# Sampling rows of four images interleaved on every fourth partition

## The chip, the cores and the metric

The kernel runs on one core of one Trainium2 chip. The metric is the device time of one execution in microseconds; the time before is the median of three runs.

## The reference, cut to what matters

A tower of vision layers over 32 images: a tokenizer made of a deformable convolution, then four pairs of attention and feed-forward layers with layer norms. Only the tokenizer matters here. Each image is cut into a 5 x 5 grid of patches of 16 x 16 points; a small convolution gives every point an offset, and the image is read at the displaced place with bilinear weights:

```python
off = _conv_offsets(x, offset_w, offset_b)            # dy, dx for 256 points of 25 patches
py = base_y[None, :, None, :] + dy
px = base_x[None, None, :, :] + dx
y0 = jnp.floor(py)
x0 = jnp.floor(px)
...
sampled = gather(y0i, x0i) * (wy0 * wx0)[..., None] + gather(y0i, x1i) * (wy0 * wx1)[..., None] + gather(y1i, x0i) * (wy1 * wx0)[..., None] + gather(y1i, x1i) * (wy1 * wx1)[..., None]
out = jnp.einsum('bhwkc,ock->bohw', sampled, Wk)
```

## The kernel before

The kernel is one program of nine stages with a barrier of all engines between them. The tokenizer is stage 0 and has three parts: `offsets` computes the places, `sample` reads the images at them, `project_and_norm` multiplies with `dconv`. The change is in `sample` and in a constant of `layout`.

`sample` writes the bilinear weight as a product of two hats, max(0, 1 - |place - row|) over the rows and the same over the columns. It goes through 40 steps: five rows of patches (`ho`) times eight tiles (`t`) of four images. A step has a window of 20 image rows for each of its four images (`WINDOW` = 20, `IMG_PER_TILE` = 4, `ROWS_Y` = 80), and each of these 80 rows is one partition. The parts of a step, by line:

- L1691, SP: the transfer of places. The y places of a row of patches, 5 x 256 numbers (5,120 B) per image, were stored to device memory by `offsets`; they are brought to the 80 partitions of `hat_y`, each image's numbers repeated for its 20 rows.
- L1696, SP: four transfers of strips, one per image: 20 rows of 3 x 84 pixels (1,008 B) each. `strip` has a slot per image in the free dimension, and image `j`'s rows fill only its own slot on its own 20 partitions; the rest stays zero from a memset at the start. So one matmul with the 80 rows as contraction keeps the four images apart.
- L1714 and L1719, ACT: the hat of y in two operations on 80 partitions. The first subtracts the row's number in its window, which is the constant `minus_row`, one number for each partition. L1717 and L1721, ACT: the same for x, after a subtraction by POOL at L1734.
- L1752, PE: 20 matmuls of hat y with the strips, into one of two sets of PSUM banks.
- L1783 and L1791, DVE: the product with the hat of x (two instructions), and the sum.

`hat_y` and `strip` have four buffers: SP waits at L1688 until the matmuls of the step four back are done, then issues the five transfers of its step, one after the other. ACT waits for the places, PE for the hat, for all four strips and for DVE to have read the bank of two steps back. Every engine has its own loop over the steps, and there is no barrier between steps. The far branch (L1698, L1703) isn't taken with these inputs.

Of the kernel before, what the change touches and what calls it, by code (L numbers as in the profile page):

```python
# [17 lines left out]
QUAD = 32  # L18
IMG_PER_TILE = 4
P = QUAD * IMG_PER_TILE  # L20
# [1468 lines left out]
GRID = 5  # L1489
TILE_TOKENS = IMG_PER_TILE * TOKENS  # L1490
KPOINTS = PATCH * PATCH
# [6 lines left out]
WINDOW = PATCH + 2 * MARGIN  # L1498
# [8 lines left out]
ROWS_Y = IMG_PER_TILE * WINDOW  # L1507
# [121 lines left out]
def sample(tw, k, w):  # L1629
# [12 lines left out]
    loads = {kind: {x: [tw.sem(f"{kind}_{x}_loaded_{p}") for p in range(BUFFERS)] for x in ("places", "pixels")} for kind in (NEAR, FAR)}  # L1642
# [12 lines left out]
    def near_or_far(eng, step, before_far=None):  # L1655

        far = eng.value_load(k.far[0:1, 0:1], min_val=0, max_val=1)
        with eng.If(far == 0):
            one_pass(eng, lambda *a: step(NEAR, *a), 0, 0, 0)
        with eng.Else():  # L1660
            if before_far:
                before_far()
            with eng.Fori(0, COVER_Y) as wy:
                with eng.Fori(0, COVER_X) as wx:
                    one_pass(eng, lambda *a: step(FAR, *a), (wy * COVER_X + wx) * (GRID * TILES), wy, wx)
# [6 lines left out]
    with tw.scratch():  # L1672
# [9 lines left out]
        with nc.psum_tensor("ps_rows", [P, 2, 4, 512], F32) as ps, nc.Block() as block:  # L1682

            @block.sync
            def _(sp):
                def step(kind, i, ho, t, p, wy, wx):
                    n = B + i + 1
                    sp.wait_ge(sems[kind]["rows_in_psum"], n - BUFFERS)  # L1688
                    version = 0 if kind == NEAR else wy + 1
                    places = k.rel_d[version].rearrange("(t j h w) c -> t h j (w c)", t=TILES, j=IMG_PER_TILE, h=GRID)[t][ho]  # L1690
                    sp.dma_start(hat_y[0:ROWS_Y, p].rearrange("q w c -> q (w c)"),  # L1691
                                 places.unsqueeze(1).to_broadcast([IMG_PER_TILE, WINDOW, GRID * KPOINTS])).then_inc(loads[kind]["places"][p], 16)
                    for j in range(IMG_PER_TILE):
                        q = slice(WINDOW * j, WINDOW * (j + 1))
                        if kind == NEAR:
                            sp.dma_start(strip[q, p, j], ins["strips"][ho][t][j]).then_inc(loads[kind]["pixels"][p], 16)  # L1696
                        else:
                            sp.dma_start(window[q, p, j], ins["windows"][wy][wx][t][j]).then_inc(loads[kind]["pixels"][p], 16)  # L1698

                def store_places():  # L1700
                    for wy in range(COVER_Y):
                        sp.wait_ge(moved, wy + 1)
                        sp.dma_start(k.rel_d[1 + wy].rearrange("(t n) c -> n t c", n=TILE_TOKENS), moved_places).then_inc(saved, 16)  # L1703
                    sp.wait_ge(saved, 16 * COVER_Y)

                near_or_far(sp, step, store_places)
# [1206 lines left out]
def layout(x):  # L2913

    a = {k: np.asarray(v) for k, v in x.items()}
    o = {}
# [3 lines left out]
    p = x[:, :, :GRID * PATCH, :GRID * PATCH].reshape(IMAGES, CHANNELS, GRID, PATCH, GRID, PATCH)  # L2920
# [16 lines left out]

    place = o["base"].reshape(TILE_TOKENS, 2, KHALVES, P)
    o["origin"] = np.concatenate([place[:, 0, 0:1, 0], place[:, 1, :, 0]], 1) - MARGIN
    o["minus_row"] = -np.resize(np.arange(WINDOW, dtype=np.float32), P)[:, None]  # L2940
    column, half = np.arange(WINDOW_X), np.arange(KHALVES)
    o["window_x"] = np.tile(HALF_COLS * half[:, None, None] + PATCH * g[:, None] - MARGIN + column, (P, 1, 1, 1)).astype(np.float32)
    o["cover_x"] = np.tile(WINDOW_X * np.arange(COVER_X)[:, None] + column, (P, 1, 1)).astype(np.float32)
# [120 lines left out]
```

## Time and profile before

| | us |
|---|---|
| median of three runs | 1320.39 (1316.8 to 1324.31) |
| time of the profiled execution | 1309.12 |
| its span | 1307.5 |
| sampling loop in it | from about 72 to 257 |

A row of a profile is a group of like instructions, a single one, or a stretch of time; the line number is that of the code above. "Idle before" is the time for which an engine stood before an instruction, with what released it. All times are microseconds unless marked ns. SPq is the sequencer of SP, which issues the transfers and computes nothing; its row of a transfer is the time for which the sequencer was taken up by the issue, not the time of the transfer.

### The profile page before, as it was taken

Reading aid. Unit: us, or ns where it says so; the run is one execution under the profiler, and the core shown is the slowest. Engines: PE = TensorE matmul, PEld = TensorE weight load, DVE = VectorE, ACT = ScalarE, POOL = GpSimd, SP = SyncE. Lnnn points to the kernel's source line nnn. Section 1 sums busy time; section 2 is a strip of 40 time slices with the busy share of each in tenths; the row PEclk is TensorE's granted clock in tenths of the full one; section 3 lists DMA queues with packets and bytes.
Section 4 is the critical chain, followed back from the end, with each engine's and each line's share of the span. In section 5 each row is a group of like instructions: output and inputs, shape, how many; then the busy total and the mean of one; then the engine's idle time right before and its main releaser. Section 6 shows DMA issues by size and latency. Waiting matters only on the chain. (4 is left out here: it accounts for less than half of the span.)

```text
span 1307.5 us, 25828 instructions
## 1 busy us (share of the span) xinstructions
PE 903.5 (69%) x9931; PEld 739.1 (57%) x9931; DVE 636.0 (49%) x1464; ACT 427.5 (33%) x728; POOL 215.1 (16%) x240
## 2 busy tenths in 40 slices
PE   4936666654656469828988557857677999476684
PEld 1335555522333359726878556646447999464573
DVE  1637777636776343166444233645463111256354
ACT  0148888512333112123334322334220111133132
POOL 2122222110000134213112001010012332100100
PEclk9969999976665579968888758968586999879598
DMA  4323333276000358010000060000052996100000
GB/s 120 83 87 113 115 114 114 79 191 145 1 0 1 98 174 204 19 49 2 2 2 2 1 156 9 4 1 3 1 133 68 225 256 144 32 2 3 1 4 20
DMA packets 63923, 90.67 MB, mean 69 GB/s; under 512 B 16532, under 2 KB 51016, under 8 KB 63824
## 3 DMA queue, kind: packets, MB, share of 16 engines
q1 hardware_dynamic: 58320, 83.57, 23.4%
q0 software_dynamic: 5504, 5.70, 2.2%
q8 instruction: 72, 1.18, 0.4%
q14 instruction: 27, 0.22, 0.1%
HBM read 81.66 MB, written 8.12 MB: 69 GB/s over the span
## 5 line engine op out<-in xcount | busy, mean ns | idle before, releaser
L1752 PE MATMUL ps_rows<-stage_strip,stage_hat_y 128*128 128x144 f32 x800 | 110.4, 294 | 73.1 <-ACT stage_hat_y L1719 73.1
L1752 PEld LDWEIGHTS ps_rows<-stage_strip,stage_hat_y 128*128 128x128 f32 x800 | 102.1, 193 | 81.4 <-ACT stage_hat_y L1719 50.1
L1783 DVE TENSOR_TENSOR stage_product<-ps_rows,stage_hat_x 128x1296 f32<-128x1296 f32 x80 | 68.9, 902 | 42.8 <-PE ps_rows L1752 42.8
L2559 DVE TENSOR_TENSOR L_ffnhid<-L_ffnact_gate,L_ffnbank_u 128x300 f32<-128x300 f32 x32 | 15.0, 467 | 117.6 <-ACT L_ffnact_gate L2577 117.6
L1791 DVE TENSOR_REDUCE stage_samples<-stage_product 128x1440 f32 x40 | 66.2, 1655 | 9.3 <-DVE stage_product L1783 9.3
L1714 ACT ACTIVATE stage_hat_y<-stage_hat_y,stage_w_minus_row 80x1280 f32<-80x1280 f32 x40 | 54.5, 1362 | 45.8 <-DMA stage_hat_y<-places_y 45.8
L1734 POOL TENSOR_TENSOR stage_hat_x<-stage_pos_xT,stage_w_window_x 128x240 f32<-128x240 f32 x80 | 48.4, 627 | 125.0 <-DVE stage_product L1783 118.9
L1556 PE MATMUL ps_conv<-stage_w_offset_w,stage_patches 128*100 128x512 f32 x96 | 44.8, 620 | 17.6 <-DMA stage_patches<-in_patchesT 17.6
L1719 ACT ACTIVATE stage_hat_y<-stage_hat_y 80x1280 f32<-80x1280 f32 x40 | 50.1, 1253 | 0.0
L1135 PE MATMUL L_attnbank_q<-L_attnhT,L_attnwq 97*128 97x200 f32 x192 | 43.6, 374 | 6.9 <-DVE L_attnqT L1298 6.7
L1135 PEld LDWEIGHTS L_attnbank_q<-L_attnhT,L_attnwq 97*128 97x128 f32 x192 | 36.8, 213 | 9.4 <-issue 8.7
L2523 PE MATMUL L_ffnbank_g<-L_ffnxT,L_ffn_win 96*128 96x100 f32 x240 | 40.7, 297 | 0.5 <-ACT L_ffnxT L2570 0.5
L2523 PE MATMUL L_ffnbank_u<-L_ffnxT,L_ffn_win 96*128 96x100 f32 x240 | 40.7, 297 | 0.0
L2492 POOL DMA_INDIRECT stage_y_rows<-L_ffndown,stage_choice_index x16 | 25.5, 1594 | 89.0 <-ACT L_ffndown L2584 89.0
L2577 ACT ACTIVATE L_ffnact_gate<-L_ffnbank_g 128x300 f32<-128x300 f32 x32 | 13.5, 421 | 80.1 <-PE L_ffnbank_u L2523 80.1
L1556 PEld LDWEIGHTS ps_conv<-stage_w_offset_w,stage_patches 128*100 128x100 f32 x96 | 16.2, 175 | 40.8 <-issue 23.1
L2343 DVE TENSOR_TENSOR L_ffnhid<-L_ffnact_gate,L_ffnbank_u 128x480 f32<-128x480 f32 x16 | 10.5, 654 | 55.4 <-ACT L_ffnact_gate L2367 55.4
L1174 PE MATMUL L_attnbank_o<-L_attnv_heads,L_attnwork 128*100 128x68 f32 x192 | 25.8, 312 | 16.1 <-ACT L_attnwork L1422 14.9
L2523 PEld LDWEIGHTS L_ffnbank_g<-L_ffnxT,L_ffn_win 96*128 96x128 f32 x240 | 35.6, 213 | 0.8 <-issue 0.8
L2523 PEld LDWEIGHTS L_ffnbank_u<-L_ffnxT,L_ffn_win 96*128 96x128 f32 x240 | 35.6, 213 | 0.0
L1174 PEld LDWEIGHTS L_attnbank_o<-L_attnv_heads,L_attnwork 128*100 128x100 f32 x192 | 24.6, 223 | 18.1 <-ACT L_attnwork L1422 16.0
L2291 PE MATMUL L_ffnbank_g<-L_ffnxT,L_ffn_win 96*128 96x240 f32 x128 | 33.0, 382 | 0.7 <-ACT L_ffnxT L2360 0.7
(430 smaller groups left out, 2176.3 us busy)
## 6 DMA issues: line engine op xcount, KB each, us to landing
stage_hat_y<-places_y SPq DMA_DIRECT2D x40, 400.0 KB
L_ffn_win<-in_L_ffn_Win SPq DMA_DIRECT2D x10, 1152.0 KB, 8.9
stage_L_ffn_win<-in_L_ffn_Win SPq DMA_DIRECT2D x6, 1152.0 KB, 9.2
L_ffnranks<-stage_ranks SPq DMA_DIRECT2D x16, 400.0 KB
L_ffn_win<-in_L_ffn_Win SPq DMA_DIRECT2D x8, 768.0 KB, 14.0
L_ffn_wout<-in_L_ffn_Wout SPq DMA_DIRECT2D x10, 576.0 KB, 6.3
stage_L_ffn_wout<-in_L_ffn_Wout SPq DMA_DIRECT2D x6, 576.0 KB, 6.5
stage_strip<-in_strips SPq DMA_DIRECT2D x160, 19.7 KB
```

The costliest lines, as they stand in the source:

```text
L1135: mm = nc.tensor.matmul(bank_q[:, i * PAIR_TOKENS:(i + 1) * PAIR_TOKENS], wq[0:rows, k, c * GROUPS + g, :], tokens, start=(k == 0), stop=( ...
L1174: mm = nc.tensor.matmul(bank_o[0:QUERIES, j // 2, at:at + OUT_COLS], work[:, t % 2, j * GROUPS + g, :], v_heads[:, t % 4, j, g, :, :], sta ...
L1556: mm = nc.tensor.matmul(ps_conv[0:TILE_TOKENS, p, :], patches[:, p, c, :], w["offset_w"][:, c, :], start=(c == 0), stop=(c == SLABS - 1))
L1714: nc.scalar.activation(y, y, ACT.Abs, bias=w["minus_row"][0:ROWS_Y, :]).then_inc(s["hat_y_abs"], 1)
L1719: nc.scalar.activation(y, y, ACT.Relu, scale=-1.0, bias=1.0).then_inc(s["hat_y"], 1)
L1734: x = nc.gpsimd.tensor_tensor(hat_x[:, p, h * GRID * IMG_PER_TILE:(h + 1) * GRID * IMG_PER_TILE, :].rearrange("q (g j) x -> q g j x", j=IM ...
L1752: mm = nc.tensor.matmul(ps[:, p % 2, bank, at * cols:(at + 1) * cols], hat_y[:, p, g, h * P:(h + 1) * P], rhs.rearrange("q j c x -> q (j c ...
L1783: last = nc.vector.tensor_tensor(split(product[:, p % 2, slots.start * cols:slots.stop * cols]), ps[:, p % 2, banks, 0:used * cols].rearra ...
L1791: nc.vector.tensor_reduce(into.rearrange("q h c w -> q h w c"), by_window, AX_X, ALU.add).then_inc(s["summed"], 1)
L2291: mm = nc.tensor.matmul(ps[:, c, f, :], weights.win[e % NB][:, k, o:o + P], xT[:, e % 2, k, :], start=(k == 0), stop=(k == 1))
L2492: nc.gpsimd.indirect_dma_start(choice.y_rows, bass.IndirectOffsetOnAxis(choice.index[0:C, e:e + 1], 0), down[:, e % RING, :], None, bounds ...
L2523: mm = nc.tensor.matmul(ps[:, c, f, :], weights.win[e % NB][:, k, o:o + P], xT[:, e % 2, k, :], start=(k == 0), stop=(k == 1))
```

## The change

The rows of the four images are interleaved: partition `4 w + j` holds row `w` of image `j`, where before it was partition `20 j + w`. In the source of the transfer of places the dimension of 20 repeats stands outside that of the four images. Each image's strip goes to every fourth partition, and `minus_row` counts 0, 0, 0, 0, 1, 1, 1, 1 and so on. `hat_y` and the slots of `strip` keep their shapes.

```diff
--- before.py
+++ after.py
@@ -1689,9 +1689,9 @@
                     version = 0 if kind == NEAR else wy + 1
                     places = k.rel_d[version].rearrange("(t j h w) c -> t h j (w c)", t=TILES, j=IMG_PER_TILE, h=GRID)[t][ho]
                     sp.dma_start(hat_y[0:ROWS_Y, p].rearrange("q w c -> q (w c)"),
-                                 places.unsqueeze(1).to_broadcast([IMG_PER_TILE, WINDOW, GRID * KPOINTS])).then_inc(loads[kind]["places"][p], 16)
+                                 places.unsqueeze(0).to_broadcast([WINDOW, IMG_PER_TILE, GRID * KPOINTS])).then_inc(loads[kind]["places"][p], 16)
                     for j in range(IMG_PER_TILE):
-                        q = slice(WINDOW * j, WINDOW * (j + 1))
+                        q = slice(j, ROWS_Y, IMG_PER_TILE)
                         if kind == NEAR:
                             sp.dma_start(strip[q, p, j], ins["strips"][ho][t][j]).then_inc(loads[kind]["pixels"][p], 16)
                         else:
@@ -2937,7 +2937,7 @@
 
     place = o["base"].reshape(TILE_TOKENS, 2, KHALVES, P)
     o["origin"] = np.concatenate([place[:, 0, 0:1, 0], place[:, 1, :, 0]], 1) - MARGIN
-    o["minus_row"] = -np.resize(np.arange(WINDOW, dtype=np.float32), P)[:, None]
+    o["minus_row"] = -np.repeat(np.arange(QUAD, dtype=np.float32), IMG_PER_TILE)[:, None]
     column, half = np.arange(WINDOW_X), np.arange(KHALVES)
     o["window_x"] = np.tile(HALF_COLS * half[:, None, None] + PATCH * g[:, None] - MARGIN + column, (P, 1, 1, 1)).astype(np.float32)
     o["cover_x"] = np.tile(WINDOW_X * np.arange(COVER_X)[:, None] + column, (P, 1, 1)).astype(np.float32)
```

The order of the instructions on every engine is the same as before. The instructions of the transfers in the built program differ in their patterns (step and number of elements of each dimension, outermost first) and, for the strips, in a field `ant_dge_precooked`, which is printed here where it is set:

```
before
L1691 out [[5120, 80], [1, 1], [1, 1280]]  in [[6400, 4], [0, 20], [1, 1280]]
L1696 out [[4032, 20], [1, 252]]           in [[252, 20], [1, 252]]            ant_dge_precooked
after
L1691 out [[5120, 80], [1, 1], [1, 1280]]  in [[0, 20], [6400, 4], [1, 1280]]
L1696 out [[16128, 20], [1, 252]]          in [[252, 20], [1, 252]]
```

All other transfers that SP issues in either program have that field set, except those of the far branch at L1698. Among them are the two of later stages that the rows below show: L2227 brings one row of 800 numbers (3,200 B) to 128 partitions, L2410 brings 128 rows of six pieces.

## Rows read from the trace of the kernel before

**Rows 1.** Busy time by stretch: the sampling loop, and 20 us in it.

```profile
core 0: us, PE busy (x) PEld busy (x) DVE busy (x) ACT busy (x) POOL busy (x), PEclk, DMA share, GB/s
...
72.00:256.00 184.00, 110.41 (x800) 102.07 (x800) 133.70 (x120) 140.32 (x160) 48.35 (x80) 0.96 0.30 107
110.00:130.00 20.00, 12.33 (x92) 11.26 (x91) 15.75 (x14) 16.85 (x19) 5.39 (x9) 1.00 0.31 114
```

**Rows 2.** Groups of the sampling loop: busy us, mean ns, idle before and releaser.

```profile
L1752 PE MATMUL ps_rows<-stage_strip,stage_hat_y 128*128 128x144 f32 x800 | 110.4, 294 | 73.1 <-ACT stage_hat_y L1719 73.1
...
L1783 DVE TENSOR_TENSOR stage_product<-ps_rows,stage_hat_x 128x1296 f32<-128x1296 f32 x80 | 68.9, 902 | 42.8 <-PE ps_rows L1752 42.8
L1791 DVE TENSOR_REDUCE stage_samples<-stage_product 128x1440 f32 x40 | 66.2, 1655 | 9.3 <-DVE stage_product L1783 9.3
L1714 ACT ACTIVATE stage_hat_y<-stage_hat_y,stage_w_minus_row 80x1280 f32<-80x1280 f32 x40 | 54.5, 1362 | 45.8 <-DMA stage_hat_y<-places_y 45.8
```

**Rows 3.** Timeline of ACT (start, duration): first step, one in the middle, last.

```profile
79.91 1.36 ACT L1714 ACTIVATE stage_hat_y<-stage_hat_y,stage_w_minus_row 80x1280 f32<-80x1280 f32 x1 [14.95 <-DMA stage_hat_y<-places_y]
...
152.87 1.36 ACT L1714 ACTIVATE stage_hat_y<-stage_hat_y,stage_w_minus_row 80x1280 f32<-80x1280 f32 x1 [0.79 <-DMA stage_hat_y<-places_y]
...
155.80 0.59 ACT L1721 ACTIVATE stage_hat_x<-stage_hat_x 128x480 f32<-128x480 f32 x1
157.17 1.36 ACT L1714 ACTIVATE stage_hat_y<-stage_hat_y,stage_w_minus_row 80x1280 f32<-80x1280 f32 x1 [0.78 <-DMA stage_hat_y<-places_y]
...
247.57 1.36 ACT L1714 ACTIVATE stage_hat_y<-stage_hat_y,stage_w_minus_row 80x1280 f32<-80x1280 f32 x1 [0.80 <-DMA stage_hat_y<-places_y]
```

**Rows 4.** DMA view of 72 to 256 us: packets and issues.

```profile
DMA packets 8167, 19.69 MB, mean 107 GB/s; under 512 B 1760, under 2 KB 4960, under 8 KB 8160
...
stage_hat_y<-places_y SPq DMA_DIRECT2D x40, 400.0 KB
stage_strip<-in_strips SPq DMA_DIRECT2D x160, 19.7 KB
```

**Rows 5.** Waits of SP in 72 to 256 us: total us, times, longest.

```profile
SPq L1691 <- PE ps_rows L1752: 40.8, 35, 2.7
```

**Rows 6.** Timeline of SP, the transfer issues at the start of the loop.

```profile
72.14 0.86 SPq L1691 DMA_DIRECT2D stage_hat_y<-places_y  x1
...
75.41 0.70 SPq L1691 DMA_DIRECT2D stage_hat_y<-places_y  x1
...
78.95 0.71 SPq L1691 DMA_DIRECT2D stage_hat_y<-places_y  x1
79.92 1.72 SPq L1696 DMA_DIRECT2D stage_strip<-in_strips  x4
81.96 0.68 SPq L1691 DMA_DIRECT2D stage_hat_y<-places_y  x1
```

**Rows 7.** Transfer issues of SP by line: count, then ns min/median/max.

```profile
L1691 SPq DMA_DIRECT2D stage_hat_y<-places_y x40: 671/677/861, 72.1 to 236.4; - x40
...
L1696 SPq DMA_DIRECT2D stage_strip<-in_strips x160: 286/286/344, 73.3 to 238.7; - x160
...
L2227 SPq DMA_DIRECT2D L_ffnranks<-stage_ranks x16: 319/428/437, 453.0 to 493.8; - x16
...
L2410 SPq DMA_DIRECT2D L_ffn_wout<-in_L_ffn_Wout x10: 367/368/3597, 763.0 to 1091.8; - x10
```

**Rows 8.** Timeline of DVE: first product, two without a wait, last product.

```profile
88.09 1.72 DVE L1783 TENSOR_TENSOR stage_product<-ps_rows,stage_hat_x 128x1296 f32<-128x1296 f32 x2 [17.91 <-PE ps_rows L1752]
...
91.55 1.71 DVE L1783 TENSOR_TENSOR stage_product<-ps_rows,stage_hat_x 128x1296 f32<-128x1296 f32 x2
...
95.09 1.71 DVE L1783 TENSOR_TENSOR stage_product<-ps_rows,stage_hat_x 128x1296 f32<-128x1296 f32 x2
...
253.45 1.72 DVE L1783 TENSOR_TENSOR stage_product<-ps_rows,stage_hat_x 128x1296 f32<-128x1296 f32 x2 [0.67 <-PE ps_rows L1752]
```

**Rows 9.** Busy time by stretch, while only four L2227 transfers run.

```profile
456.00:458.00 2.00, 0.00 (x0) 0.00 (x0) 0.00 (x0) 0.00 (x0) 0.00 (x0) 0.50 0.91 230
```

## The prediction

> **What bounds the kernel now.** I read four views of the sampling loop, the only place where the change acts, in this order: the stretches, the groups, the DMA view, and the issues of SP.
>
> The stretches say where the loop lies and that no engine in it is full: 184 us, of which ACT is busy 140.3 and DVE 133.7, and from 110 us on TensorE holds its full granted clock [rows 1]. The groups say who waits for whom: DVE waits for PE (42.8 us), PE for ACT's hat of y (73.1), and ACT's first operation of a step, L1714, waits in all 40 steps for the transfer of places (45.8) [rows 2]. The timeline of ACT gives the beat: L1714 starts at 79.91 in the first step and at 247.57 in the last, so a step is 167.66 / 39 = 4.30 us. ACT's four operations end 3.52 us after L1714 starts (155.80 + 0.59 - 152.87), and then it stands 0.78 us until the next transfer has landed [rows 3]. So the transfers of places set the beat.
>
> Why does one need 4.30 us? The transfer at L1691 brings 80 rows of 5,120 B and the four of L1696 bring 20 rows of 1,008 B each. Over 40 steps that is 3,200 and 3,200 data packets. The DMA view counts 8,160 under 8 KB and 4,960 under 2 KB, which fits with 1,760 left over, all under 512 B [rows 4]. 1,760 = 40 x 4 + 160 x 10: one closing packet for each DMA engine that takes part, if a transfer of places runs on 4 engines and a strip on 10. I know no other split that fits (40a + 160b = 1,760 with a and b dividing the 20 rows or the 4 images). The load agrees: at a share of 0.31 of 16 engines [rows 1] a step has 0.31 x 16 x 4.30 = 21.3 engine-us; four engines busy all the time are 17.2 of them, and the other 4.1 on six engines are 0.7 each, which is the strips' part. On the four engines places then take 4.30 - 0.7 = 3.6 us, 0.18 us a packet.
>
> [...]
>
> **The change, part by part.**
>
> *Transfer of places.* Its outer dimension becomes 20. If it runs on 10 engines, as the strips with 20 rows do, each takes 8 of its packets: 8 x 0.18 = 1.44 us, with the strips 2.1 us a step on each engine. The DMA engines no longer bound anything. The first transfer lands 12 x 0.18 = 2.1 us earlier. From its issue at 72.14 [rows 6] to L1714 at 79.91 [rows 3] were 7.8 us; 5.7 remain.
>
> *Next in line: DVE.* Where it had no wait its steps were 3.46 us (88.09 to 91.55) and 3.54 (91.55 to 95.09) [rows 8]; with ACT at about 3.5 the loop could run at 3.52.
>
> *Next in line: SP.* SP issues five transfers a step and waits 40.8 us in 35 waits for PE to free a buffer [rows 5], 1.17 us a step. Its own work is therefore 4.30 - 1.17 = 3.13 us; the one steady interval without a wait, 78.95 to 81.96, is 3.01 [rows 6]. This is only 1.17 us below the present beat, and less than DVE's 3.52 by 0.4.
>
> *Strips.* And here the change takes something away. Their destination was 20 neighbouring partitions; it becomes every fourth. In the built program the four strip transfers lose the field `ant_dge_precooked`, which all SP transfers but L1691's and the unused far branch's carry. The number of bytes, rows and instructions is the same, the form of the issue isn't. The trace has prices for both forms, though for different shapes: L1696 with the mark costs SP 286 ns, L1691 without it 677 [rows 7]. Lower bound: nothing, 286 stays. Upper bound: 677, so 0.39 us more for each strip. How much of the 0.39 is shape? [...] That leaves 0.25 us for the mark, and I take it: 4 x 0.25 = 1.00 us a step. The transfer of places was unmarked and stays so; for six more engines I add the 0.03 between the marked 286 and 319.
>
> SP's step is then 3.13 + 1.00 + 0.03 = 4.16 us. That is more than DVE's 3.52, so SP sets the beat. Its first two intervals were longer than its own 3.13, by 0.14 and 0.41 (3.27 and 3.54 [rows 6]); I keep 0.5.
>
> The last L1714 starts at 72.14 + 39 x 4.16 + 0.5 + 5.7 = 240.6 instead of 247.57: 7.0 us earlier. What follows it (8.5 us to the end of the loop, then the projection) is unchanged.
>
> *The rest.* ACT's bias per row is another table of the same size, the matmuls contract over the same 80 rows in another order, no instruction moves on any engine: nothing. PE would run at the same clock and wait.
>
> **Sum.** The profiled execution took 1309.12 us; less 7.0 is 1302.1. The median of the three timed runs is 11.3 us above that execution, so the forecast on their scale is 1320.4 - 7.0 = 1313.4 us, 0.5% faster. A measurement of this kernel can tell about 0.5% (6.6 us) from no change.
>
> **The rivals.**
>
> *A. The mark costs nothing on SP.* Then DVE sets the beat at 3.52. The first product starts 2.1 us earlier, at 86.0, the last at 86.0 + 39 x 3.52 = 223.3 instead of 253.45 [rows 8]: 30.2 us, 1290 us. For it: SP's time shows no dependence on the mark alone, since no two rows have one shape. Against: 286 and 677 are the two ends of all SP issues in the loop, and they are split by exactly this. [...]
>
> *B, on the other side: strips cost what L1691 costs.* Place: SP's sequencer at L1696. Price: 0.39 x 4 = 1.56 us, a step of 4.72, last L1714 at 72.14 + 184.1 + 0.5 + 5.7 = 262.4, 14.9 us later than now: 1335 us. It decides from the point where 72.14 + 39T + 6.2 passes 247.57, T = 4.34, which is 0.295 us more for each strip. For it: 677 is the only unmarked price the trace has. Against: L1691 has a third level and four times the rows.
>
> *C. The transfer stays on 4 engines.* Then the DMA beat of 4.30 remains, unless SP's is longer: 1320 us. Against: 10 engines for the strips' 20 rows.
>
> *D. Ten engines that read the same 20 KB get in each other's way.* The worst row: while only transfers that repeat one row of 3,200 B for 128 partitions run, 0.91 of 16 engines move 230 GB/s [rows 9], 15.8 B a ns each. A packet of places would take 0.32 us, eight 2.6 us, with strips 3.3: still under 4.16. To reach 4.30 it would have to be 0.45. So this costs up to 1 us at the first landing and no more; the time is the forecast's.
>
> **How the numbers follow.** Cases by the extra time of a strip issue: none or nearly (A): 0.11, about 1290. From 0.05 to 0.25 us: 0.37, times from 1295 to 1313. From 0.25 to 0.34: 0.29, within 0.5% of no change. Above: 0.20, to 1335 (B). C: 0.03. The forecast's own case, 0.20 to 0.30 us, has 0.40 of it all, and its own range is steps of 3.96 to 4.36, 1306 to 1321 us. For 8 in 10 I cut half of A and a third of B, and allow 3 us for the spread of the runs: 1292 to 1333. Faster by over 0.5%: 0.48; within: 0.31; slower: 0.21.
>
> **What would show it.** In the changed profile: packets under 512 B in the loop 40 x 10 + 160 x 10 = 2,000 (1,760 if C). The mean of L1696's issues at about 0.54 us (0.29 for A, 0.68 for B), that of L1691 at about 0.7. SP's wait for PE gone, where now it is 1.17 us a step; if it is still there and ACT no longer waits for DMA, A. L1714 of the first step at about 77.8. Steps of 4.16 us. ACT's idle time would still be put down to DMA, although the DMA engines are idle more, because a transfer issued late lands late: the DMA share stays near 21 / (16 x 4.16) = 0.32. The prediction is wrong if the strips' issue is off by more than 0.05 us, since each 0.05 is 0.2 us a step and 7.8 us in all; that is the number on which everything hangs.

## The result and the profile after

The changed kernel takes 1350.78 us (median of 4 runs, 1350.23 to 1354.24) against 1322.35 for the kernel before: ratio 1.0271, 95% interval 1.0225 to 1.0317. This ratio isn't the quotient of the two medians, which are 28.4 us apart and give 1.0215. The kernel is thus 2 to 3% slower, where 0.5% faster was forecast.

The issues of SP by line (count, then ns min/median/max), as in [rows 7]:

```profile
L1691 SPq DMA_DIRECT2D stage_hat_y<-places_y x40: 803/803/1025, 72.3 to 272.7; - x40
...
L1696 SPq DMA_DIRECT2D stage_strip<-in_strips x160: 727/741/772, 73.7 to 276.5; - x160
```

The strip issue is the number to read: 741 ns, where it was 286. The places' issue rose too, from 677 to 803. SP's timeline at the start of the loop (start, duration), as in [rows 6]:

```profile
72.35 1.02 SPq L1691 DMA_DIRECT2D stage_hat_y<-places_y  x1
...
77.62 0.80 SPq L1691 DMA_DIRECT2D stage_hat_y<-places_y  x1
...
83.11 0.80 SPq L1691 DMA_DIRECT2D stage_hat_y<-places_y  x1
84.16 3.55 SPq L1696 DMA_DIRECT2D stage_strip<-in_strips  x4
88.04 0.80 SPq L1691 DMA_DIRECT2D stage_hat_y<-places_y  x1
```

In this interval SP needs 4.93 us from one transfer of places to the next (83.11 to 88.04), where the steady one before took 3.01; the interval in front of it is longer (77.62 to 83.11, 5.49), and so the mean of the loop will be too. Within a step one strip's issue follows the other after (3.55 - 0.741) / 3 = 0.936 us; before it was (1.72 - 0.286) / 3 = 0.478. SP's waits in the whole loop:

```profile
engine line waited for: us in total, times, longest us
SPq L1682 <- PEq L1682: 11.5, 1, 11.5
```

The wait for PE at L1691, 40.8 us before [rows 5], is gone; what is left is the barrier at the end. So SP never stands: it sets the beat. The timeline of ACT, first step, last step, and the first instruction after the barrier at the loop's end:

```profile
77.69 1.36 ACT L1714 ACTIVATE stage_hat_y<-stage_hat_y,stage_w_minus_row 80x1280 f32<-80x1280 f32 x1 [12.54 <-DMA stage_hat_y<-places_y]
...
278.15 1.36 ACT L1714 ACTIVATE stage_hat_y<-stage_hat_y,stage_w_minus_row 80x1280 f32<-80x1280 f32 x1 [1.54 <-DMA stage_hat_y<-places_y]
...
289.36 1.28 ACT L1899 ACT_TABLE_LOAD   x1 [7.70 <-PEq L1682]
```

A step is (278.15 - 77.69) / 39 = 5.14 us, before 4.30 [rows 3]. The first L1714 starts 2.2 us earlier than before, as was expected of the faster transfer.

A second reading tells whether SP or the DMA engines set a beat: the time from the issue of a transfer of places to the L1714 that needs it. Before it was 7.8 us in the first step (72.1 to 79.91) and 11.2 in the last (236.4 to 247.57), so transfers queued up behind each other. Now it is 5.3 (72.35 to 77.69) and 5.5 (272.7 to 278.15): nothing queues up, and a transfer comes late only because it is issued late. The groups and two stretches of the loop (columns of the stretches as in [rows 1]):

```profile
L1752 PE MATMUL ps_rows<-stage_strip,stage_hat_y 128*128 128x144 f32 x800 | 136.9, 340 | 78.4 <-ACT stage_hat_y L1719 78.4
...
L1783 DVE TENSOR_TENSOR stage_product<-ps_rows,stage_hat_x 128x1296 f32<-128x1296 f32 x80 | 68.8, 901 | 75.4 <-PE ps_rows L1752 75.4
...
L1714 ACT ACTIVATE stage_hat_y<-stage_hat_y,stage_w_minus_row 80x1280 f32<-80x1280 f32 x40 | 54.5, 1362 | 76.2 <-DMA stage_hat_y<-places_y 76.2
```

```profile
72.00:289.36 217.36, 136.85 (x800) 128.48 (x800) 133.94 (x120) 140.32 (x161) 48.34 (x81) 0.81 0.38 91
110.00:130.00 20.00, 13.05 (x77) 12.22 (x76) 12.83 (x13) 13.06 (x17) 4.46 (x8) 0.83 0.41 98
```

ACT's wait is still put down to the transfer of places, now 76.2 us; DVE waits 75.4 for PE. TensorE's granted clock in those 20 us is 0.83 where it was 1.00, and a matmul takes 340 ns where it took 294. Between steps that costs nothing, since SP is late anyway; only the last step's chain, from L1714 to the end of the loop, takes 11.2 us where it took 9.8. The DMA view tells that the number of engines changed as planned:

```profile
DMA packets 8405, 19.67 MB, mean 95 GB/s; under 512 B 2000, under 2 KB 5200, under 8 KB 8400
```

2,000 packets under 512 B are 40 x 10 + 160 x 10: places now run on ten DMA engines. The records of the single packets agree: from the first to the last packet of places four were under way in 137 of 173 us before; now, of the 108 us in which any is under way, ten are in 75.

The loop ends at 289.36 instead of 257.37, 32.0 us later: 39 x 0.84 for the steps, less 2.2 at the first, and 1.4 more behind the last. The two profiled spans differ by 41.1. The other 9.1 us lie behind the loop, where nothing was changed: from the loop's end to the end of the span were 1050.1 us before and 1059.2 after, and in the traces of the runs below between 1051 and 1066. This time goes roughly with TensorE's granted clock, read from 700 to 1100 us: 1050 and 1051 us in the two traces with 0.80, 1055 to 1062 in the seven with 0.79, 1059 (the changed kernel's) and 1063 in the two with 0.78 and 1065.5 in the one with 0.77. Why the clock differs there was not tried. The loop's part, 32.0 us or 2.4%, is what the rest of this document explains; it lies between the 2.15% of the medians and the 2.7% of the ratio.

### The profile page after: what moved, and what is told of

It reads as the page before. It is cut to its first block and busy times, and to the rows that moved or that the text cites. A ratio compares the mean times of both kernels' runs of the same rounds, so it can differ in the third digit from the quotient of the medians.

```text
span 1348.6 us, 25828 instructions
## 1 busy us (share of the span) xinstructions
PE 945.3 (70%) x9931; PEld 777.4 (58%) x9931; DVE 635.2 (47%) x1464; ACT 427.4 (32%) x728; POOL 215.1 (16%) x240
## 5 line engine op out<-in xcount | busy, mean ns | idle before, releaser
L1752 PE MATMUL ps_rows<-stage_strip,stage_hat_y 128*128 128x144 f32 x800 | 136.9, 340 | 78.4 <-ACT stage_hat_y L1719 78.4
L1752 PEld LDWEIGHTS ps_rows<-stage_strip,stage_hat_y 128*128 128x128 f32 x800 | 128.5, 234 | 86.7 <-ACT stage_hat_y L1719 50.0
L1783 DVE TENSOR_TENSOR stage_product<-ps_rows,stage_hat_x 128x1296 f32<-128x1296 f32 x80 | 68.8, 901 | 75.4 <-PE ps_rows L1752 75.4
L1714 ACT ACTIVATE stage_hat_y<-stage_hat_y,stage_w_minus_row 80x1280 f32<-80x1280 f32 x40 | 54.5, 1362 | 76.2 <-DMA stage_hat_y<-places_y 76.2
```

The costliest lines, as they stand in the source:

```text
L1714: nc.scalar.activation(y, y, ACT.Abs, bias=w["minus_row"][0:ROWS_Y, :]).then_inc(s["hat_y_abs"], 1)
L1752: mm = nc.tensor.matmul(ps[:, p % 2, bank, at * cols:(at + 1) * cols], hat_y[:, p, g, h * P:(h + 1) * P], rhs.rearrange("q j c x -> q (j c ...
L1783: last = nc.vector.tensor_tensor(split(product[:, p % 2, slots.start * cols:slots.stop * cols]), ps[:, p % 2, banks, 0:used * cols].rearra ...
```

## The experiments

Theory M: the transfer of places alone would have freed the loop, but the strips lost the mark (the field `ant_dge_precooked`), and SP's issue time took over the beat.

**The mark alone.** The kernel before, with

```diff
+                            nc.dge_precook = False
                             sp.dma_start(strip[q, p, j], ins["strips"][ho][t][j]).then_inc(loads[kind]["pixels"][p], 16)
+                            nc.dge_precook = True
```

> The kernel before, with the strip transfers' destinations as they were (20 neighbouring partitions) and only the mark taken from their instructions; the transfer of places stays on 4 engines. Theory M (the lost mark): the strip issues go from 0.29 to about 0.74 us although nothing in their pattern changed, SP's step is 3.13 + 4 x 0.455 = 4.95 us, its wait for PE is gone, the last L1714 comes some 25 us later: ratio to the kernel before 1.019. Rival S (the stride): it is the step of four partitions that makes the issue or the write dear; here there is none, so the issue stays at 0.29, the step at 4.30, ratio 1.00.

Measured: 1349.64 us, ratio 1.0247 (1.0212 to 1.0283). Issues, and ACT's first and last step (the line of L1714 is L1716 here):

```profile
L1691 SPq DMA_DIRECT2D stage_hat_y<-places_y x40: 699/699/868, 70.9 to 268.7; - x40
...
L1697 SPq DMA_DIRECT2D stage_strip<-in_strips x160: 727/745/810, 72.1 to 272.5; - x160
```

```profile
78.51 1.36 ACT L1716 ACTIVATE stage_hat_y<-stage_hat_y,stage_w_minus_row 80x1280 f32<-80x1280 f32 x1 [14.75 <-DMA stage_hat_y<-places_y]
...
276.16 1.36 ACT L1716 ACTIVATE stage_hat_y<-stage_hat_y,stage_w_minus_row 80x1280 f32<-80x1280 f32 x1 [0.80 <-DMA stage_hat_y<-places_y]
```

The strip issue costs 745 ns with the old partitions, the step is 197.65 / 39 = 5.07 us (4.95 expected, and a ratio of 1.019). A loss of the same size comes with the mark alone; the stride of four partitions isn't needed for it. Rival S falls. That unmarked strips make the DMA engines late, and not SP, is excluded by the time from issue to L1716: 7.6 us in the first step (70.9 to 78.51) and 7.5 in the last (268.7 to 276.16), where it grew to 11.2 in the kernel before.

**Places alone.**

```diff
-                                 places.unsqueeze(1).to_broadcast([IMG_PER_TILE, WINDOW, GRID * KPOINTS])
+                                 places.unsqueeze(0).to_broadcast([WINDOW, IMG_PER_TILE, GRID * KPOINTS])
```

> The kernel before with only the pattern of the places transfer changed (20 outside 4); strips and minus_row are as before, so the hats are computed from rows of the wrong image and the output isn't the reference's. Theory M: the strips keep their mark, SP's step is 3.13 + 0.13 = 3.26 us, the places run on 10 engines, and DVE sets the beat at about 3.52 us: 30 us faster, ratio 0.977. Packets under 512 B in the loop: 2,000. Rival T (the transfer on ten engines is itself no faster, since all read the same 20 KB): steps of 4.3 us or more, ratio 1.00 or above.

Measured: 1284.89 us, ratio 0.9737 (0.9704 to 0.9769). Issues, SP's wait, 20 us of the loop (columns as in [rows 1]), ACT's first and last step:

```profile
L1691 SPq DMA_DIRECT2D stage_hat_y<-places_y x40: 812/814/1020, 72.4 to 206.5; - x40
...
L1696 SPq DMA_DIRECT2D stage_strip<-in_strips x160: 286/287/424, 73.8 to 209.0; - x160
```

```profile
SPq L1691 <- PE ps_rows L1752: 4.1, 13, 0.4
```

```profile
150.00:170.00 20.00, 15.05 (x113) 14.08 (x113) 18.55 (x18) 20.00 (x25) 7.28 (x12) 1.00 0.57 138
```

```profile
77.76 1.36 ACT L1714 ACTIVATE stage_hat_y<-stage_hat_y,stage_w_minus_row 80x1280 f32<-80x1280 f32 x1 [12.47 <-DMA stage_hat_y<-places_y]
...
212.18 1.35 ACT L1714 ACTIVATE stage_hat_y<-stage_hat_y,stage_w_minus_row 80x1280 f32<-80x1280 f32 x1
```

The step is 134.42 / 39 = 3.45 us, and ACT is busy 20.00 of 20 us: ACT sets the beat, a little below the 3.52 that I had read from DVE. The transfer on ten engines is worth 33 us. SP has almost nothing to spare: with 4.1 us of waits in all, 0.1 a step, its own work is about 3.35 us. Nor have the DMA engines: a share of 0.57 of 16 is 9.1 engines, if all of this runs on the same ten.

**Strips alone.** The changed kernel with the places transfer of before.

> The changed kernel with the places transfer as before (4 outside 20): strips on every fourth partition, unmarked; the hats meet rows of the wrong image, so the output isn't the reference's. Theory M: SP's step is that of the changed kernel less what the places issue gained, 5.14 - 0.13 = 5.01 us, L1691's issue is back at 0.68, ratio to before about 1.02. Theory S predicts the same time; together with e1 it tells the two apart. Rival U (places on ten engines and strips get in each other's way in the changed kernel): the step falls to about 4.3, ratio 1.00.

Measured: 1350.19 us, ratio 1.0236 (1.0188 to 1.0284).

```profile
L1691 SPq DMA_DIRECT2D stage_hat_y<-places_y x40: 699/699/868, 71.1 to 268.9; - x40
...
L1696 SPq DMA_DIRECT2D stage_strip<-in_strips x160: 727/745/810, 72.3 to 272.7; - x160
```

The step is 5.08 us (first L1714 at 78.60, last at 276.61), again with no growing queue (7.5 us from issue to L1714 in the first step, 7.7 in the last). Same as with the mark alone, stride or no stride. In the changed kernel ten engines instead of four thus make no difference to the time, since SP is the bound.

**What decides the price of an unmarked issue?** In the kernel before, only the row count of strips 1 to 3 was changed, so that they should run on 1, 16 and 10 engines; first with the mark (in this and the later cuts of code, `...` stands for what is left out, such as the branches and the semaphores):

```diff
-                            sp.dma_start(strip[q, p, j], ins["strips"][ho][t][j]) ...
...
+                            sp.dma_start(strip[WINDOW:2 * WINDOW - 1, p, 1], ins["strips"][ho][t][1][0:WINDOW - 1]) ...
...
+                            sp.dma_start(strip[2 * WINDOW:2 * WINDOW + 16, p, 2], ins["strips"][ho][t][2][0:16]) ...
...
+                            sp.dma_start(strip[3 * WINDOW:3 * WINDOW + 10, p, 3], ins["strips"][ho][t][3][0:10]) ...
```

> The kernel before; of the strips of images 1, 2 and 3 only 19, 16 and 10 of the 20 rows are brought (the missing pixels are left out of the result), each with a line of its own, all marked. 19 rows should run on 1 DMA engine, 16 on 16, 10 and 20 on 10. Read: the issue's price by engines in the marked form. Theory K (SP pays for each engine that it feeds): 0.006 us an engine, as between 0.286 on 10 and 0.319 on 16: 20 rows 0.29, 19 rows 0.23, 16 rows 0.32, 10 rows 0.29. Rival R (it pays by rows): falling from 20 to 10. The time stays near that of before.

Measured, in the order of 20, 19, 16 and 10 rows:

```profile
L1696 SPq DMA_DIRECT2D stage_strip<-in_strips x40: 300/300/344, 72.8 to 263.1; - x40
...
L1698 SPq DMA_DIRECT2D stage_strip<-in_strips x40: 229/230/249, 73.3 to 263.6; - x40
...
L1700 SPq DMA_DIRECT2D stage_strip<-in_strips x40: 321/2155/3708, 73.8 to 264.0; - x40
...
L1702 SPq DMA_DIRECT2D stage_strip<-in_strips x40: 286/286/335, 74.3 to 266.5; - x40
```

With the mark the issue goes by engines: 0.23 us for one, 0.29 to 0.30 for ten, 0.32 at least for sixteen. The median of 2.16 at sixteen is a stall of the issue, and the time (one run) was 1348.92 us, against my expectation: the step is 4.995 us, with SP almost never waiting for PE (1.6 us in all). Here the transfers do queue up: from the issue of places to ACT's first operation are 7.8 us in the first step (71.7 to 79.49) and 12.1 in the last (262.2 to 274.31). My estimate is that the one DMA engine that carries the 19 rows has the most work. If it also carries a quarter of the places and its part of the other strips, that is 20 packets of places at a median of 0.196 us and 2 + 19 + 1 + 1 = 23 of strips at 0.046, 4.98 us a step. What makes SP's issue stall was not shown.

The same with the mark taken from the strip transfers, as in the first experiment:

> The same four row counts with the mark taken from the strip transfers (pixels of images 1 to 3 left out as there). Theory K: the price in the unmarked form is a base and 0.021 us an engine, as between L1691's 0.677 on 4 engines and 0.803 on 10: 20 rows 0.74, 19 rows (1 engine) 0.55, 16 rows (16 engines) 0.87, 10 rows 0.74. Rival R (rows): 0.74, 0.73, 0.70, 0.64. Packets under 512 B in the loop: 40 x (4 + 10 + 1 + 16 + 10) = 1,640.

Measured (one run, 1355.97 us), same order:

```profile
L1697 SPq DMA_DIRECT2D stage_strip<-in_strips x40: 750/752/812, 72.9 to 266.6; - x40
...
L1699 SPq DMA_DIRECT2D stage_strip<-in_strips x40: 616/620/636, 73.9 to 267.6; - x40
...
L1701 SPq DMA_DIRECT2D stage_strip<-in_strips x40: 549/562/1602, 74.8 to 268.4; - x40
...
L1703 SPq DMA_DIRECT2D stage_strip<-in_strips x40: 795/801/811, 75.5 to 269.5; - x40
```

Here too the transfers queue up (7.5 us from issue to ACT in the first step, 71.7 to 79.15, and 11.6 in the last, 265.7 to 277.32), so this run's time says nothing of SP's part in it; only its issues are read. Four more row counts, in the same way:

> As the unmarked run with four row counts, now with 8, 12, 18 and 5 rows (8, 12, 9 and 5 DMA engines; the other pixels are left out of the result). So far unmarked: 0.55 us on 16 engines, 0.62 on 1, 0.75 and 0.80 on 10, which no straight line in engines or rows fits. Theory N (a number of engines that is a power of two is cheap): 8 rows about 0.58, the other three 0.7 to 0.8. Theory H (the price has a hump in the middle): 8, 9, 12 and 5 all between 0.65 and 0.8, without a step between 8 and 9.

Measured (one run, 1338.89 us), in the order of 8, 12, 18 and 5 rows:

```profile
L1697 SPq DMA_DIRECT2D stage_strip<-in_strips x40: 670/671/698, 72.6 to 265.3; - x40
...
L1699 SPq DMA_DIRECT2D stage_strip<-in_strips x40: 745/751/772, 73.5 to 266.2; - x40
...
L1701 SPq DMA_DIRECT2D stage_strip<-in_strips x40: 746/748/787, 74.4 to 267.1; - x40
...
L1703 SPq DMA_DIRECT2D stage_strip<-in_strips x40: 702/704/716, 75.4 to 268.1; - x40
```

The packets under 512 B in this loop are 1,520 = 40 x (4 + 8 + 12 + 9 + 5), which fits these numbers of engines. By DMA engines the unmarked issue costs 0.62 (1), 0.70 (5), 0.67 (8), 0.75 (9), 0.75 to 0.80 (10), 0.75 (12) and 0.56 us (16). Theory K's straight line is refuted (it asked for 0.55 on 1 and 0.87 on 16), and so is rival R by rows: 10 rows cost more than 20. N and H both miss as stated: eight engines cost 0.67 and not 0.58, and there is a step of 0.08 between 8 and 9 where H allowed none. What is left of N, that 1, 8 and 16 engines (0.56 to 0.67) are cheaper than 5, 9, 10 and 12 (0.70 to 0.80), fits every row of the strips, but the numbers of rows and of engines were changed together in these runs. Why sixteen is so cheap stays open.

**Sixteen rows in the changed kernel.**

```diff
-                            sp.dma_start(strip[q, p, j], ins["strips"][ho][t][j]) ...
+                            sp.dma_start(strip[j:16 * IMG_PER_TILE:IMG_PER_TILE, p, j], ins["strips"][ho][t][j][0:16]) ...
```

> The changed kernel with 16 of the 20 rows of each strip brought (the last four rows of each window are left out of the result), still on every fourth partition and unmarked, so that each strip runs on 16 engines. The issue should fall from 0.74 to about 0.56 us, SP's step from 5.14 by 4 x 0.18 to about 4.4 us, so the kernel comes back to near the time before: ratio 1.00 to 1.01. If instead the stride holds the loop up, or the number of rows has no part in it, the step stays near 5.1 and the ratio at 1.02 to 1.03.

Measured: 1313.27 us, ratio 0.9973 (0.9936 to 1.0011).

```profile
L1691 SPq DMA_DIRECT2D stage_hat_y<-places_y x40: 834/838/1027, 71.9 to 235.9; - x40
...
L1696 SPq DMA_DIRECT2D stage_strip<-in_strips x160: 495/496/584, 73.3 to 239.1; - x160
```

Still strided, still unmarked, but 0.50 us an issue instead of 0.74 (0.56 expected); the step falls to (241.10 - 77.88) / 39 = 4.19 us, and the loss is gone. The cheaper issues alone give 5.14 - 4 x 0.245 = 4.16. The edit also brings a fifth fewer strip rows, on 16 engines instead of 10, but nothing queued up in the changed kernel (5.3 and 5.5 us from issue to L1714), so less to transfer could not have moved the beat.

**Other ways to get the gain.** One strip transfer with its zeros from device memory, in the changed layout:

```diff
-                    for j in range(IMG_PER_TILE):
-                        q = slice(j, ROWS_Y, IMG_PER_TILE)
...
-                            sp.dma_start(strip[q, p, j], ins["strips"][ho][t][j]) ...
...
+                        sp.dma_start(strip[0:ROWS_Y, p], ins["wide_strips"][ho][t]) ...
```

> The changed kernel with the four strip transfers of a step made one: the strips lie in device memory with their zeros, 80 rows of 4,032 B, and one marked transfer brings them to 80 neighbouring partitions. SP issues two transfers a step instead of five: about 0.80 + 0.26 + 0.35 + 0.35 = 1.8 us of its own, so it waits for PE again. Places on 10 engines take 1.44 us, strips on up to 16 engines 5 packets each, some 0.7 us. Theory M: DVE sets the beat at about 3.52, 30 us faster than before, ratio 0.977. Rival: four times the strip bytes (323 KB a step) make the DMA engines the bound, steps above 4 us, ratio 0.99 to 1.00.

Measured: 1302.57 us, ratio 0.9893 (0.9846 to 0.9940). SP's wait, and 20 us of the loop:

```profile
SPq L1691 <- PE ps_rows L1752: 74.7, 36, 5.3
```

```profile
150.00:170.00 20.00, 15.28 (x116) 14.21 (x116) 17.82 (x18) 18.91 (x22) 6.35 (x11) 1.00 0.80 196
```

SP waits again, 36 times and 2.1 us each time, and the step is (229.48 - 77.95) / 39 = 3.89 us, not 3.52. The rival named the right bound, though its steps were to be above 4 us: in this trace a packet of places takes 0.33 us on average and one of the wide strips 0.28. If places run on ten engines and strips on sixteen (1,040 packets under 512 B fit that), an engine that carries both needs 8 x 0.33 + 5 x 0.28 = 4.0 us a step. Four times the strip bytes use up most of what the ten engines gave.

With the old partitions, the places in four marked transfers:

```diff
...
+                    for j in range(IMG_PER_TILE):
+                        sp.dma_start(hat_y[WINDOW * j:WINDOW * (j + 1), p].rearrange("q w c -> q (w c)"),
+                                     places[j:j + 1].to_broadcast([WINDOW, GRID * KPOINTS])).then_inc(loads[kind]["places"][p], 16)
```

> The kernel before with the partitions as they were and the places brought by four transfers, one per image: 20 repeats each, marked, on 10 engines. SP issues eight marked transfers a step: 8 x 0.478 + 0.33 = 4.15 us and no unmarked one. Theory M (the mark and the number of issues set SP's step): 4.15 against 4.30, 6 to 8 us faster, ratio 0.995. Rival (ten engines alone give the gain): 3.45 us as with places changed alone, ratio 0.974.

Measured: 1306.39 us (10 runs), ratio 0.9943 (0.9913 to 0.9972).

```profile
76.24 1.36 ACT L1715 ACTIVATE stage_hat_y<-stage_hat_y,stage_w_minus_row 80x1280 f32<-80x1280 f32 x1 [11.75 <-DMA stage_hat_y<-places_y]
...
237.54 1.36 ACT L1715 ACTIVATE stage_hat_y<-stage_hat_y,stage_w_minus_row 80x1280 f32<-80x1280 f32 x1 [0.25 <-DMA stage_hat_y<-places_y]
```

161.30 / 39 = 4.14 us a step, 4.15 expected: eight marked issues, each 0.478 us behind the one before it, and 0.33 for the rest. And with the strips of two images in one transfer as well (`pair_strips`, 40 rows of 2,016 B, twice a step):

> As the last, and the strips brought by two transfers instead of four: 40 rows of two images with the zeros between them from device memory, 2,016 B a row. SP issues six marked transfers: 6 x 0.478 + 0.33 = 3.2 us, under ACT's 3.45. The strip bytes are 161 KB a step, half those of the single wide transfer. Theory M: ACT sets the beat, 3.45 to 3.6 us, ratio 0.975 to 0.98. Rival: the DMA engines bound it as with the wide transfer, 3.9 us, ratio 0.99.

Measured: 1285.07 us, ratio 0.9796 (0.9728 to 0.9863).

```profile
150.00:170.00 20.00, 15.06 (x113) 13.96 (x112) 18.56 (x18) 20.00 (x25) 7.25 (x12) 1.00 0.59 165
```

```profile
77.69 1.36 ACT L1717 ACTIVATE stage_hat_y<-stage_hat_y,stage_w_minus_row 80x1280 f32<-80x1280 f32 x1 [12.04 <-DMA stage_hat_y<-places_y]
...
212.05 1.35 ACT L1717 ACTIVATE stage_hat_y<-stage_hat_y,stage_w_minus_row 80x1280 f32<-80x1280 f32 x1
```

ACT is full, the step is 134.36 / 39 = 3.45 us. This version computes all that the kernel before does and is faster than both kernels, by 2.0% than the one before and by some 4.6% than the changed one (0.9796 / 1.0271 = 0.954, from two sets of runs).

## Why the prediction was wrong

- *The transfers of places on four DMA engines bound the loop*: right. With places alone changed the time is 33 us shorter, and the packet count moved from 1,760 to 2,000 with the engines. Every count fits one packet under 512 B for each engine of a transfer, with 10 engines for 20 rows, and 1, 16 and 10 for 19, 16 and 10 rows (1,640 in both of those runs, as expected). These counts are sums over all transfers; the engines of a single strip transfer were not read by themselves.
- *The first transfer lands 2.1 us earlier*: 77.69 against 77.8 forecast.
- *Ten engines, 2.1 us a step on each, packets of 0.18 us*: wrong, without weight in the changed kernel. In its trace a packet of places takes 0.32 us on average (0.20 before), so an engine needs 8 x 0.32 + 8 x 0.08 = 3.2 us a step. That is Rival D's price almost to the digit (0.32 a packet, 3.3 a step). D was right, too, that it decides nothing at SP's beat; but with places alone changed (0.32 a packet again) it lies only 0.2 us under ACT's 3.45. For the same reason the DMA share came out at 0.38 over the loop; the 21 engine-us that the forecast put into 0.32 would give 0.26 at steps of 5.14 us. That the ten engines disturb each other over the same 20 KB, as D has it, was not tried.
- *SP next in line, 3.13 us of its own*: right. 3.13 + 4 x 0.455 + 0.126 = 5.08 us, measured 5.14.
- *The strips lose the mark, and SP sets the beat*: right as a mechanism, shown by the kernel with the mark alone removed.
- *0.25 us for each strip, at most 0.39*: the step that failed, and the term that was mis-sized. It is 0.455 (741 ns less 286), above even the upper bound. Of the 37.5 us by which the last L1714 comes later than forecast (278.15 against 240.6), this term is 39 x 4 x 0.205 = 32. I had taken L1691's 677 ns as a ceiling because its pattern is larger, and then taken 0.14 of the 0.39 off for shape, an amount that no run shows: with the pattern left as it was and the mark alone taken off, the issue rose by 0.459 us (745 ns less 286). But L1691 ran on four DMA engines and the strips on ten, and I had not asked what that is worth in the unmarked form. L1691 itself went to 803 ns with ten. Seen so, the strips' 741 is 677, with 126 more for the engines and 62 less for shape. This split isn't clean: L1691's pattern changed with its engines, and shape counts in its own right, since on ten engines each 10 rows cost 0.80 us and 20 rows 0.75. On sixteen engines the extra would have been 0.18 to 0.24 (0.50 or 0.56 less the marked 0.32), near my 0.25.
- *0.03 us for the places' issue on ten engines*: 0.126. Here I did go by engines, but at the marked form's price of 0.006 us an engine (L2227's least issue of 319 ns [rows 7] less 286, over six engines).
- *DVE's 3.52 as the floor*: it is ACT's 3.45. This had no weight. In the chances, 1295 us does not follow for 0.05 us more a strip: SP's step would be 3.36 us, under that floor, and the time Rival A's 1290.
- *PE at the same clock*: its granted clock fell from 1.00 to 0.83, which in the loop shows only in the 1.4 us behind the last step.
- Rival B had the right sign, place and mechanism with 4.72 us a step; with 5.14 it missed by 39 x 0.42 = 16 us. The range stopped short of even its time.

## What to carry to other kernels

A change of layout for the sake of one transfer can change the form of its neighbours' issue, as the strips' went from 286 to 741 ns here: compare the built instructions of every transfer on the queue, fields included, and not only their order and size. When an engine's sequencer has little slack (1.17 us a step for four issues: 0.29 us each here), an unknown price that is bounded by a row of another engine count isn't bounded. To tell a late issue from a slow transfer, compare the time from issue to use in the first and the last step: it grew from 7.8 to 11.2 us where transfers queued up, and stood at 5.3 and 5.5 where SP was late. Where one transfer must run on more engines, splitting it can leave the layout, and so its neighbours' mark, alone. The split costs more issues (here 4 x 0.478 = 1.9 us a step in place of one unmarked issue of 0.8 us), and pays in full only if they are won back elsewhere, as the paired strips did.

## What was not expected of the hardware

The unmarked issue's price over the number of DMA engines doesn't rise evenly (0.62 us on 1, 0.75 to 0.80 on 9 to 12, 0.50 to 0.56 on 16), while the marked one, read on 1, 10 and 16, rises from 0.23 over 0.29 to 0.32 at least. The DMA engines' busy time isn't a property of the packets alone: for the same 8,160 packets a step took 0.31 x 16 x 4.30 = 21.3 engine-us before, and 0.35 x 16 x 5.07 = 28 with the strips unmarked; with places on ten engines (8,400 packets) 0.57 x 16 x 3.45 = 31. There it is the places' own packets of 5,120 B that grow, from 0.20 us on average to 0.32. What makes them dearer wasn't tried.
